# Two slots of 16 pairs in place of three for a streamed adjacency matrix, ScalarE's loop written out, the last stores on ScalarE's queue

## The reference

```python
keep = (u >= 0.1).astype(x.dtype)
x_drop = x * keep / (1.0 - 0.1)
x = layernorm(x + jnp.matmul(adj, x_drop), axis=-1)   # x, u: 8192 x 64, adj: 8192 x 8192, all f32
```

## Time and profile before

| | us |
|---|---|
| runs | 645.14, 645.23, 646.56 (median 645.23) |
| profiled execution | 645.01 |
| its span | 643.2 |
| TensorE busy | 511.4 (80%) |
| VectorE, ScalarE, GpSimd busy | 48.6, 30.1, 18.0 |
| DMA: share of the 16 engines, mean rate | 99.4%, 427 GB/s |
| mean granted TensorE clock | 0.931 of full |

### The profile page before, as it was taken

The page is one execution under the profiler, slowest core; times in us unless marked ns, Lnnn a source line. Parts: engine busy times, 40 slices in busy tenths (PEclk is TensorE's granted clock), DMA queues, the critical chain, the costliest instruction groups (busy, mean ns, idle before and its releaser), DMA issues.

```text
span 643.2 us, 5701 instructions
## 1 busy us (share of the span) xinstructions
PE 511.4 (80%) x2308; PEld 176.4 (27%) x2308; DVE 48.6 (8%) x230; ACT 30.1 (5%) x33; POOL 18.0 (3%) x27
## 2 busy tenths in 40 slices
PE   0396887879879877987778888878787878789896
PEld 0131322223223322222222222322222222223326
DVE  3100101010010100101010010101001010000102
ACT  0000001010010101001010100101001010100001
POOL 0000000000000000000000000000000000000000
PEclk9998898888898998898988978979988988989998
DMA  9999999999999999999999999999999999999997
GB/s 376 422 452 436 430 421 441 429 422 444 445 419 437 441 412 438 428 447 419 451 441 413 437 430 427 436 453 425 434 433 434 417 441 448 419 419 432 428 423 290
DMA packets 9962, 274.80 MB, mean 427 GB/s; under 512 B 1388, under 2 KB 1642, under 8 KB 2666
## 3 DMA queue, kind: packets, MB, share of 16 engines
q1 hardware_dynamic: 9960, 274.76, 99.4%
HBM read 272.66 MB, written 2.10 MB: 427 GB/s over the span
## 4 chain that ended last, share of the span: by engine, by line
DMA 70%; PE 27%; issue 2%; SPq 0%; DVE 0%; POOL 0%; POOLq 0%; ACT 0%; DVEq 0%; ACTq 0%
DMA raw<-adj_dram 70%; PE acc L175 27%; PE turned L195 0%; SPq L128 0%; POOL rstd L263 0%; DVE stats L233 0%; POOLq L47 0%; ACT sums L213 0%; DVE rows L229 0%; SPq L133 0%; SPq L132 0%; SPq L131 0%; DVE moments L238 0%; POOLq L268 0%; DVE final_normed L256 0%
## 5 line engine op out<-in xcount | busy, mean ns | idle before, releaser
L175 PE MATMUL acc<-raw,dropped 128*64 128x504 f32 x2048 | 484.5, 633 | 77.4 <-POOLq L268 76.1
L175 PEld LDWEIGHTS acc<-raw,dropped 128*64 128x64 f32 x2048 | 151.8, 147 | 398.0 <-issue 289.9
L229 DVE TENSOR_TENSOR rows<-turned,x_sb 126x256 f32<-126x256 f32 x16 | 6.8, 424 | 553.0 <-PE turned L195 553.0
L213 ACT ACT_TABLE_LOAD x16 | 20.5, 1283 | 598.9 <-PE acc L175 598.9
L195 PE MATMUL turned<-join,sums 128*126 128x64 f32 x128 | 18.0, 285 | 32.6 <-ACT sums L213 32.6
L263 POOL TENSOR_TENSOR rstd<-var_eps,minus_half 126x4 f32<-126x4 f32 x16 | 16.2, 1013 | 615.2 <-DVE var_eps L241 578.5
L195 PEld LDWEIGHTS turned<-join,sums 128*126 128x126 f32 x128 | 15.8, 194 | 46.5 <-ACT sums L213 46.5
L244 DVE TENSOR_SCALAR normed<-rows,moments,rstd 126x64 f32 x64 | 15.7, 310 | 20.1 <-POOL rstd L263 20.1
L185 PE MATMUL final_turned<-x_final,eye 128*128 128x64 f32 x2 | 0.7, 447 | 17.9 <-DVE dropped L224 17.9
L233 DVE BATCH_NORM_STATS2 stats<-rows 126x6 f32<-126x64 f32 x64 | 9.7, 213 | 0.6
L213 ACT COPY sums<-acc 128x504 f32<-128x504 f32 x16 | 9.3, 579 | 0.2
(11 more groups left out here) (14 smaller groups left out, 2.6 us busy)
## 6 DMA issues: line engine op xcount, KB each, us to landing
raw<-adj_dram SPq DMA_DIRECT2D x30, 5544.0 KB, 27.0
raw<-adj_dram SPq DMA_DIRECT2D x14, 5040.0 KB, 29.1
raw<-adj_dram SPq DMA_DIRECT2D x2, 3024.0 KB, 21.3
raw<-adj_dram SPq DMA_DIRECT2D x2, 2520.0 KB, 26.9
raw<-adj_dram SPq DMA_DIRECT2D x2, 2016.0 KB, 22.8
raw<-adj_dram SPq DMA_DIRECT2D x2, 1512.0 KB, 26.1
dropped<-u_dram SPq DMA_DIRECT2D x1, 2048.0 KB, 7.6
x_sb<-x_dram SPq DMA_DIRECT2D x1, 2048.0 KB, 12.1
```

The costliest lines, as they stand in the source:

```text
L175: last = nc.tensor.matmul(sum_bank[t * D:(t + 1) * D, 0:width], dropped[:, t * PAIRS + q, :], raw[:, s, start:start + width], start=(q == ...
L213: nc.scalar.copy(sums[:, :], acc[:, 0:WIDTH]).then_inc(sums_ready, 1)
L229: nc.vector.tensor_tensor(rows[:, :, :], turned[0:ROWS, 0:GROUPS, :], x_sb[0:ROWS, bass.ds(b * GROUPS, GROUPS), :], ALU.add).then_inc(turn ...
```

## The change

The slots become two of 16 pairs, with rows of 64,512 bytes in each partition. `PARTS` is cut anew, so that the last slot of block 14 has five parts, the first slot of block 15 three and the second five. ScalarE's loop over blocks is written out by Python, so its program has 16 copies in a straight line. The stores of block 15 and the store of the final part are issued by ScalarE in place of SP. ScalarE waits for block 15's `normed_ready`, issues its two stores, then waits for the final product, copies it, waits for its normalised rows and stores them. SP stores blocks 0 to 14 and waits for all four block stores.

```diff
-SLOT_PAIRS = [(0, 11), (11, 22), (22, 32)]
+SLOT_PAIRS = [(0, 16), (16, 32)]
 SLOTS = len(SLOT_PAIRS)
 SLOT = max(q1 - q0 for q0, q1 in SLOT_PAIRS) * PAIR
-PARTS = [(0, 0, 6), (0, 6, 11), (1, 11, 17), (1, 17, 22), (2, 22, 26), (2, 26, 29), (2, 29, 31), (2, 31, 32)]
+PARTS = [(0, 0, 6), (0, 6, 11), (0, 11, 16), (1, 16, 22), (1, 22, 26), (1, 26, 29), (1, 29, 31), (1, 31, 32)]
...
+        def store_blocks(engine, p0, p1, b0, b1):
+            engine.dma_start(out_dram[p0:p1, b0 * GROUPS * D:b1 * GROUPS * D],
+                             normed[p0:p1, b0 * GROUPS:b1 * GROUPS, :]).then_inc(blocks_stored, DMA)
...
-            stores = 0
-            for b0, b1 in [(0, BLOCKS - 1), (BLOCKS - 1, BLOCKS)]:
-                sp.wait_ge(normed_ready, b1)
-                for p0, p1 in [(0, EVEN), (EVEN, ROWS)]:
-                    sp.dma_start(out_dram[p0:p1, b0 * GROUPS * D:b1 * GROUPS * D],
-                                 normed[p0:p1, b0 * GROUPS:b1 * GROUPS, :]).then_inc(blocks_stored, DMA)
-                    stores += 1
-            sp.wait_ge(normed_ready, BLOCKS + 1)
-            sp.dma_start(out[ROWS * CHUNKS:N, :], final_normed[:, :]).then_inc(final_stored, DMA)
-            sp.wait_ge(blocks_stored, stores * DMA)
-            sp.wait_ge(final_stored, DMA)
+            sp.wait_ge(normed_ready, BLOCKS - 1)
+            for p0, p1 in [(0, EVEN), (EVEN, ROWS)]:
+                store_blocks(sp, p0, p1, 0, BLOCKS - 1)
+            sp.wait_ge(blocks_stored, 4 * DMA)
...
-            with act.Fori(0, BLOCKS) as b:
+            for b in range(BLOCKS):
                 act.wait_ge(multiplied, b * SLOTS + SLOTS)
 
                 act.wait_ge(turned_free, b + 1)
                 nc.scalar.copy(sums[:, :], acc[:, 0:WIDTH]).then_inc(sums_ready, 1)
+
+            act.wait_ge(normed_ready, BLOCKS)
+            for p0, p1 in [(0, EVEN), (EVEN, ROWS)]:
+                store_blocks(act, p0, p1, BLOCKS - 1, BLOCKS)
             act.wait_ge(final_multiplied, 1)
             nc.scalar.copy(final_sums[:, :], final_acc[:, 0:P]).then_inc(final_sums_ready, 1)
+            act.wait_ge(normed_ready, BLOCKS + 1)
+            act.dma_start(out[ROWS * CHUNKS:N, :], final_normed[:, :]).then_inc(final_stored, DMA)
+            act.wait_ge(final_stored, DMA)
```

## The result

The changed kernel takes 657.35 us (median of 4 runs, 653.23 to 660.95) against 645.18 for the kernel before (645.09 to 646.56): a ratio of 1.0192, interval 1.0147 to 1.0237. It is slower by 1.9%, where a gain of 0.5% was forecast. Its runs differ far more from each other than those of before, the slower ones on the whole at the lower mean granted clock: 653.23 us at 0.920, 657.19 at 0.905, 657.51 at 0.908, 660.95 at 0.897. The profile is of the fastest of them (653.23, span 651.3), so it shows the loss at its smallest.

The account below looks back on a forecast made before the run. The load stream was taken as the bound, TensorE's chain as setting the end. Terms -2.8 (table load and clock), +0.2 (last store), -0.4 (rows) gave -3.0 on 645.01: 642.0, 642.2 as median; own range 641.0 to 643.0, 8 in 10 up to 645.2.

Parts of the forecast that it names:

- The step that failed: Load stream with two slots: refills move 18.1 us after a landing at worst, the other slot lasts until 19.07; cost 0.
- Rival B: Load stream: a refill reaches an engine after 19.07 us and the stream breaks; 0.3 us at 28 refills, 650.6 us; chance 0.10.
- The sign that was to show it: Load stream: landings over 19.1 us apart, refill issued less than 1.3 us before the other slot is drained.
- The Trainium skill's rule: TensorE: long gaps between bursts of matmuls drop the clock; every slot starts low, charged 2.8 us a slot, sum unchanged.
- ScalarE written out and the clock at the end: After block 15: table load gone (-1.28 us) and clock stays high; gain 2.8 us, clipped by the last load.
- The drain that the prediction quotes: ScalarE's table load: the skill puts a drain of about 1.38 us beside it; the prediction expected none to be saved.
- After it: From TensorE's end to the span's end: unchanged, but the last store's issue is ScalarE's; 0.2 us added.
- Rows of 63 KB: Loads of blocks 0 to 13: two rows a partition in place of three, 112 fewer an engine; gain of 0.4 us.
- C: Load rows: longer rows move worse, +3.4 us in place of -0.4, 646.0 us; chance 0.04.
- D: ScalarE's copies: the table load stays in each, the end is as before, 645.0 us; chance 0.06.
- A: The end: only the table load is gained, as the clock falls or stores hold things up; 643.9 us; chance 0.20.

Follow-up runs that it names:

- s3_scalar: Kernel before, with its three slots, plus only the ScalarE part of the change (loop written out, last stores on ScalarE's queue): 642.96 us, ratio 0.9963.
- s2_warm_trim: Changed kernel plus spare matmuls: 5 and 2 a block in blocks 0 to 13, 12 before the first slot: 644.04 us, ratio 0.9997 to the kernel before.
- s2_only: Kernel before with only the two slots of 16 pairs, ScalarE's loop and SP's stores as before: 660.47 us, ratio 1.0248.
- s2_less4: Changed kernel with 4 of 32 pairs of each block not multiplied, output not the reference's: 649.26 us, ratio 1.0076 to the kernel before.
- s2_half: Changed kernel with 12 of 32 pairs of each block not multiplied, all loads kept, output not the reference's: 642.54 us, ratio 0.9955 to the kernel before.
- s3_straight: Kernel before with only ScalarE's loop written out, all stores still on SP: 642.78 us, ratio 0.9975.
- s3_late: Three slots with the ScalarE part, each refill in the loop waiting until the slot behind it is multiplied too: 681.04 us, ratio 1.0575 to the kernel before.
- s3_straight_again: Kernel before with only ScalarE's loop written out, measured once more on the same chip: 642.91 us, ratio 0.9974.

## Why the prediction was wrong

**The step that failed** is "The other slot keeps the engines fed until 19.07. The margin is 1.0 to 3.8 us ... I put this part at 0". TensorE's own terms held: 13.74 us at the high clock (13.8 forecast), at most 16.51 after the first slot (16.6 charged), 0.18 to the issue (0.15). At 16.24 the refill was issued 2.9 us before the other slot's landing, inside my margin with 1.25 us for moving data, and still 1.2 us were lost. The step's price of 0 measured as 11.3 us over 28 distances, and TensorE's end on block 15 came 10.2 us later than in `s3_scalar` (its copy starts at 637.04 against 626.88).

What was wrong in it can be read from the records of single packets in the traces. A row of 64,512 bytes takes its engine 2.38 us (the median of 3,712), and eight rows an engine are the 19.05 us of a slot. For the refill issued at 128.52 the first row starts at 129.47, 0.95 us later, so my 0.75 to 1.25 us for the path held. But the engines do not stay fed until the landing: the first of them has finished its last row at 128.2, 2.9 us before the slot is passed on, and at 129.4 fourteen of the 16 have none. And the 16 rows with which they start again take 2.5 to 4.1 us. A stretch with just these 16 rows (length; last the clock, the share of the engines, GB/s) and one with the 16 first rows of a refill in `s2_warm_trim`:

```profile
129.40:131.10 1.70, 0.00 (x0) 0.00 (x0) 0.00 (x0) 0.00 (x0) 0.00 (x0) 0.91 1.89 607
...
317.00:319.40 2.40, 1.03 (x3) 0.14 (x1) 0.00 (x0) 0.00 (x0) 0.00 (x0) 1.00 1.00 430
```

The view counts a packet's whole time where it starts, so 1.89 x 1.70 = 3.2 us and 1.00 x 2.40 = 2.4 us are the mean times of these rows. Over blocks 0 to 13 and the first slot of block 14, the time over 2.38 us a row and the time without a packet come, for an engine, to:

| run | slow rows, us | no packet, us |
|---|---|---|
| changed kernel | 8.1 | 3.6 |
| `s2_only` | 10.1 | 5.6 |
| `s2_less4` | 5.9 | 0.8 |
| `s2_warm_trim` | 1.2 | 0.1 |
| `s2_half` | 0.9 | 0.1 |

8.1 + 3.6 = 11.7 is about the 11.3 us of the distances. So two thirds of the loss are rows that take longer where a late refill joins, also where hardly an engine runs dry: around the refill of `s2_less4` issued at 375.13, 4.3 us ahead, 25 rows took up to 4.4 us and 1.0 us was lost. Why such rows take longer no run here shows. A landing is the last of 16 engines, so a delay counts only as far as it hits the latest of them; that may be why equal leads lose unequally, which is argued and not shown.

**Rival B was this mechanism**, with the right evidence ("an engine that runs dry starts poorly") and a chance of 0.10. Its price, 28 x 0.3 = 8.4 us, was near the measured 10 to 11; that is luck, since its condition (TensorE's time and the path over 18.1 by 1.0) never came about and its 0.3 us was no measured price. The sign that was to show it, an issue less than 1.3 us before the other slot is drained, did not come either, counted to the landing: the leads were 2.2 us and more. Its 650.6 lies below all four runs.

**The Trainium skill's rule** of the prediction ("TensorE: Matmul & The Clock Gate", "Why this matters for your kernels") bears on this loss, and the trace agrees with it: 24 of the 28 whole slots up to 577.38 took 15.1 to 16.7 us in place of 13.74. With the clock held up the same two slots lose nothing in the stream (644.04 against 657.35). I had charged the low clock at its worst, but weighed it against a margin that was not there.

**ScalarE written out and the clock at the end:** right. TensorE's way from block 15 to the end of the final part shrank by 2.9 us (forecast 2.8), with the turn at 1.09 and the final matmuls at 7.27 in place of 8.28 (6.9 forecast). The drain that the prediction quotes from the Trainium skill ("ScalarE: Activation LUTs", "What ACT_TABLE_LOAD costs") is not to be seen here either: the gap before the turn shrank from 2.04 to 0.68 us, by 1.36, little more than the load's own 1.28.

**After it:** mis-sized. I charged 0.2 us for the last store on ScalarE's queue; it cost 0.9, since it landed after 2.4 us in place of 1.5. Its queue is not the reason. On SP's queue it took 2.1 us in `s3_straight` (1.5 before), on ScalarE's 1.5 in `s2_warm_trim` (first and second line):

```profile
out_dram<-final_normed SPq DMA_DIRECT2D x1, 32.0 KB, 2.1
...
out_dram<-final_normed ACTq DMA_DIRECT2D x1, 32.0 KB, 1.5
```

It goes with the stores of blocks 0 to 14. In the microsecond before its issue the engines moved 284 GB/s in the changed kernel and 155 in `s3_straight`, but 28 in `s2_warm_trim` and none in the kernel before. An end that comes earlier after the last loads meets these stores, and part of the gain goes.

**Rows of 63 KB:** right in sign and size. 14 blocks x (38.14 - 38.10) = 0.6 us against 0.4, although the bound behind it was miscalculated: the two equations give c = -0.02 us, and errors of 0.01 us move it from -0.04 to +0.01. Rivals C and D fell with `s2_half` and the one table load. Of A, the clock did not fall; the last store was held up, but not by its own queue.

## What to carry to other kernels

The margin of a double buffer is not from landing to landing. Count it from the refill's issue to the moment the other transfer lands, and ask for some 5 us where transfers of 8 MB move at 430 GB/s (below 4.5 us the refills of two 16-pair slots lost up to 2 us each); the same memory cut into four slots gives it for 0.16 us a block (38.26 against 38.10). A DMA share of 98.9% does not say that the stream is whole: compare the distances of landings with what the bytes need. And before a consumer's time is put beside such a margin, look at what the wait does to its clock.

## What was not expected of the hardware

A stream that is refilled with little lead loses more than the time it is empty: 0.5 to 1.9 us at leads of 2.2 to 2.9 us before the landing, 2.1 us at 0.7 (`s3_late`). The rows at the joint take up to 4.1 us in place of 2.38.

The consumer's clock sets the lead: 16-pair slots that run partly at the low clock after a wait take 15.1 to 16.7 us, those at the high one throughout 13.74. The loss does not feed on itself, though, since a late landing gives the next refill more lead (2.6 us and 1.85 lost at 380.81, then 5.3 us and 0.15 lost). That the slower runs have the lower mean clock (0.920 to 0.897, 653 to 661 us) fits, but which comes first there isn't shown.

The times of the kernel before fall into groups, among the 21 taken beside `s3_straight_again` 643.2 to 643.8, 644.6 to 645.4 and 646.3 to 646.7, where the kernel with ScalarE's loop written out stays within 642.4 to 643.5. The fall of the clock after 2.04 us of standing still at the end, which cost 1.5 us against the turn and the final matmuls of the changed kernel (1.63 + 8.28 in the earlier trace rows, 1.09 + 7.27 after), may be what divides them; this was argued from one profile, not shown.

Spare f32 matmuls that all write the same half of a PSUM bank took 0.39 us each per instruction of 448 columns (3.92 us for 10), where the kernel's own, which change halves at each tile, took 0.215 for 504 (13.74 us for 64). That the halves are the reason isn't shown.
